# Residual rows by GpSimd gathers, and a register-addressed expert weight, in a two-stage attention and expert kernel

## The reference

```
x = x + delta_attention(layernorm(x))      # 16 heads of 8, a recurrence over the 512 tokens
x = x + experts(layernorm(x))
x = x + linear_attention(layernorm(x))     # 16 heads, chunks
x = x + experts(layernorm(x))

delta_attention:  q, k, v = silu(short_conv(x @ W)); q, k normalised per head
                  per token: v' = (v - k.S) * beta;  S += k (x) v';  o = q.S
                  o normalised per head, then @ Wo
experts:          gate = the two largest of softmax(x @ Wg), scaled to sum 1
                  y = sum over 8 experts of gate_e * (relu(x @ W1[e]) @ W2[e])   # 128 -> 256 -> 128
```

## Time and profile before

| | us |
|---|---|
| median of 3 runs (lowest, highest) | 939.39 (935.42, 940.16) |
| the profiled execution | 939.41 |
| its span | 937.6 |
| TensorE busy | 768.9 |
| VectorE busy | 645.5 |
| ScalarE busy | 540.8 |
| GpSimd busy | 394.9 |

### The profile page before, as it was taken

The page is one execution under the profiler, slowest core; times in us unless marked ns, Lnnn a source line. Parts: engine busy times, 40 slices in busy tenths (PEclk is TensorE's granted clock), DMA queues, the critical chain, the costliest instruction groups (busy, mean ns, idle before and its releaser), DMA issues.

```text
span 937.6 us, 17223 instructions
## 1 busy us (share of the span) xinstructions
PE 768.9 (82%) x5736; PEld 630.8 (67%) x5736; DVE 645.5 (69%) x1477; ACT 540.8 (58%) x1457; POOL 394.9 (42%) x433
## 2 busy tenths in 40 slices
PE   2653455888888899686888999999999999999997
PEld 1432233676666677574776787878787878787886
DVE  1146999899999999989854456565666574748350
ACT  5656446777877959464647454454535363636355
POOL 1065978597978889785561111111101010101012
PEclk9776667999999999789799999999999999999999
DMA  4223040403122030401010000000000000000000
GB/s 125 72 68 82 1 115 0 116 1 93 35 67 59 11 104 1 115 1 57 1 46 1 24 1 24 1 22 0 22 0 22 0 22 0 22 0 12 2 12 12
DMA packets 48446, 32.15 MB, mean 34 GB/s; under 512 B 37520, under 2 KB 38800, under 8 KB 48144
## 3 DMA queue, kind: packets, MB, share of 16 engines
q1 hardware_dynamic: 48400, 31.58, 12.1%
HBM read 18.73 MB, written 12.85 MB: 34 GB/s over the span
## 4 chain that ended last, share of the span: by engine, by line
PE 44%; DVE 28%; issue 8%; ACT 7%; POOL 5%; DMA 4%; SPq 2%; DVEq 0%; ACTq 0%; POOLq 0%
PE bank L1095 14%; PE bank L1241 6%; DVE u L1404 4%; PE bank L1073 4%; DVE hist_mem L1705 4%; DVE hist_mem L1413 4%; PE bank L1218 4%; PE bank L1075 3%; PE bank L1074 3%; DVE prod_mem L1397 3%; DVE hist_mem L1409 3%; POOL kk L473 2%; PE bank L1253 2%; DMA beta_p<-s_beta 2%; DVE x L1547 1%
## 5 line engine op out<-in xcount | busy, mean ns | idle before, releaser
L1095 PE MATMUL bank<-w,hid 128*128 128x128 f32 x2048 | 266.5, 286 | 30.5 <-DVE x L1547 9.0
L1095 PEld LDWEIGHTS bank<-w,hid 128*128 128x128 f32 x2048 | 256.9, 201 | 45.6 <-issue 33.1
L537 POOL TENSOR_TENSOR x_odd<-x_odd,y_odd 128x512 f32<-128x512 f32 x48 | 61.7, 1286 | 411.4 <-ACT y_odd L775 411.4
L740 ACT ACTIVATE hid<-bank 128x512 f32<-128x512 f32 x256 | 144.0, 600 | 97.1 <-PE bank L1075 94.2
L1073 PE MATMUL bank<-xT_h,w_h 128*128 128x512 f32 x256 | 115.2, 450 | 2.2 <-ACT hid L740 1.7
L1075 PE MATMUL bank<-xT_h,w_l 128*128 128x512 f32 x256 | 101.9, 398 | 0.0
L1074 PE MATMUL bank<-xT_l,w_h 128*128 128x512 f32 x256 | 101.6, 397 | 0.0
L522 POOL TENSOR_TENSOR oq_mem<-hist_mem,q_t 128x384 f32<-128x384 f32 (+1 forms) x96 | 101.4, 1089 | 0.0
L1404 DVE TENSOR_REDUCE u<-prod_mem 128x32 f32<-128x288 f32 x128 | 87.0, 679 | 3.3
L1005 PE MATMUL bank<-xnT_h,wtap_h 128*128 128x512 f32 x104 | 51.9, 499 | 35.3 <-DVE qkv L1369 21.1
L1712 DVE TENSOR_TENSOR prod_mem<-bank,causal 128x1024 f32<-128x1024 f32 x32 | 39.2, 1225 | 55.0 <-PE bank L1218 53.9
(11 more groups left out here) (169 smaller groups left out, 1501.8 us busy)
## 6 DMA issues: line engine op xcount, KB each, us to landing
s_qkv<-qkv SPq DMA_DIRECT2D x24, 256.0 KB, 3.6
pin<-s_qkv SPq DMA_DIRECT2D x16, 256.0 KB, 2.9
x_in<-in_x SPq DMA_DIRECT2D x8, 256.0 KB, 2.7
q_p<-s_qkv SPq DMA_DIRECT2D x8, 256.0 KB, 3.2
s_o<-o_p SPq DMA_DIRECT2D x8, 256.0 KB, 2.1
x_r<-in_x SPq DMA_DIRECT2D x8, 256.0 KB, 3.0
o_T<-s_o SPq DMA_DIRECT2D x8, 256.0 KB, 3.6
s_x<-x_odd SPq DMA_DIRECT2D x8, 256.0 KB, 2.4
```

What stands on the lines that cost most here:

```text
L740: nc.scalar.activation(hid[:, e % 2, f], bank[:, ZB + f, :], ACT.Relu).then_inc(hid_ready, 1)
L1095: last = nc.tensor.matmul(bank[:, y_bank(e, wide), tokens], hid[:, e % 2, f, tokens], w2[:, e, f], start=(f == 0), stop=(f == FC - 1))
```

## The change

The load of `x_r` for chunks 0 to 6 leaves SP. GpSimd issues four indirect transfers in its place, one for each block j of 128 rows, in a new function `fetch_residual`. Each takes its 128 row numbers from a column of the tile `row_at`, which an iota fills at the start. The call stands in GpSimd's step after `delta_solve(i + 1)` and before `delta_outputs(i, 0)`. `out_residual` waits for the four transfers of its chunk (argument `close`). The last chunk's `x_r` is still loaded by SP, on a semaphore of its own, `xr_last`. GpSimd's loop over steps 2 to 6 is written out.

In `moe_down` with `wide=False` TensorE first loads the expert's number from the tile `expert_at` in SBUF, filled by a second iota, into a register; the slice of `w2` is then addressed by that register. The values are the same as before: the number loaded for expert e is e. The semaphore `pool_ready` counts two more operations.

```diff
--- before.py
+++ after.py
@@ -178,6 +178,8 @@
 
         x_b = sb("x_b", [128, J, D])
         x_keep = x_in
+        row_at = sb("row_at", [128, NCH, J], mybir.dt.int32)
+        expert_at = sb("expert_at", [128, E], mybir.dt.int32)
         phi_min = sb("phi_min", [128, 2, NT])
         phi_k = sb("phi_k", [128, B, 2, CH])
 
@@ -239,7 +241,7 @@
 
         o_squared, o_norms, o_log = sem("o_squared"), sem("o_norms"), sem("o_log")
         o_rnorm, on_ready, o_projected = sem("o_rnorm"), sem("on_ready"), sem("o_projected")
-        xr_loaded = sem("xr_loaded")
+        xr_loaded, xr_last = sem("xr_loaded"), sem("xr_last")
 
         xr_ready, bnf_done, mvf_ready = sem("xr_ready"), sem("bnf_done"), sem("mvf_ready")
         rstdf_log, rstdf_ready, xf_ready = sem("rstdf_log"), sem("rstdf_ready"), sem("xf_ready")
@@ -270,7 +272,7 @@
                    (wv_b[:], d["wv_b"]), (wo_b[:], d["wo_b"]), (bo_rows[:], d["bo_rows"])]
         PREP_W = 5
 
-        POOL_ALL = 10
+        POOL_ALL = 12
         HALF = CH // 2
         FIRST = [i * (BS - 1) - i * (i - 1) // 2 for i in range(BS)]
         PRE_OPS = 2 + (BS - 1) + 2 * (BS - 1)
@@ -357,13 +359,14 @@
                 sp.wait_ge(go, 1)
                 if due(added_to):
                     sp.wait_ge(added, added_to)
-                sp.dma_start(x_r[:].rearrange("p j d -> p (j d)"), d["x"][c]).then_inc(xr_loaded, 16)
+                sp.dma_start(x_r[:].rearrange("p j d -> p (j d)"), d["x"][c]).then_inc(xr_last, 16)
 
             def heads_out(c):
 
                 heads_store(c)
                 heads_load(c)
-                load_xr(c)
+                if c == NCH - 1:
+                    load_xr(c)
 
             def store_mid(c):
                 this = held(sp, EV * (c + 1))
@@ -406,8 +409,6 @@
                     heads_store(o)
                 if i >= 3:
                     store_mid(i - 3)
-                if i:
-                    load_xr(o)
                 if ahead:
                     q_in(i + 1)
                 if i:
@@ -451,6 +452,11 @@
             pool.wait_ge(pool_ready, 8)
             for par in range(2):
                 nc.gpsimd.memset(v_bd[64 * par:64 * par + 64, :, :, par, HD], 1.0).then_inc(pool_ready, 1)
+
+            pool.wait_ge(pool_ready, 10)
+            nc.gpsimd.iota(row_at[:], pattern=[[128 * J, NCH], [1, J]], base=0, channel_multiplier=J).then_inc(pool_ready, 1)
+            pool.wait_ge(pool_ready, 11)
+            nc.gpsimd.iota(expert_at[:], pattern=[[1, E]], base=0, channel_multiplier=0).then_inc(pool_ready, 1)
 
             tt = nc.gpsimd.tensor_tensor
 
@@ -529,6 +535,16 @@
                 rows = oq.rearrange("p n j m d -> p (n j m) d")
                 tt(rows[:, :, HD // 2:HD], rows[:, :, 0:HD // 2], rows[:, :, HD // 2:HD], ALU.add).then_inc(o_part, 1)
 
+            def fetch_residual(c):
+
+                pool.wait_ge(pool_ready, POOL_ALL)
+                if c > 1:
+                    pool.wait_ge(added, EV * (c - 1) + 1)
+                for j in range(J):
+                    nc.gpsimd.indirect_dma_start(
+                        x_r[:, j], None, d["x"].rearrange("c p (j d) -> (c p j) d", j=J),
+                        bass.IndirectOffsetOnAxis(ap=row_at[:, c, j:j + 1], axis=0)).then_inc(xr_loaded, 16)
+
             def moe_add(n, e):
 
                 pool.wait_ge(odd_scaled, EV * n + e // 2 + 1)
@@ -549,6 +565,8 @@
                 if ahead:
                     delta_keys(i + 1)
                     delta_solve(i + 1)
+                if i:
+                    fetch_residual(i - 1)
                 delta_outputs(i, 0)
                 if moe:
                     moe_add(n, 3)
@@ -570,7 +588,7 @@
                 nc.gpsimd.memset(column[:, :, BS - 1, :, HD], 0.0).then_inc(oq_cleared, 1)
             step1(0, moe=False)
             step1(1, moe=False)
-            with pool.Fori(2, NCH - 1) as i:
+            for i in range(2, NCH - 1):
                 step1(i)
             step1(NCH - 1, ahead=False)
 
@@ -1077,6 +1095,7 @@
 
             def moe_down(n, e, wide=True, first=False):
 
+                at = e if wide else pe.value_load(expert_at[0:1, e:e + 1], min_val=0, max_val=E - 1)
                 pe.wait_ge(hid_ready, FC * (E * n + e + 1))
                 if e % 2 == 0 and wide and not first:
                     pe.wait_ge(even_scaled, scaled_even(n) + e // 2)
@@ -1092,7 +1111,8 @@
                 for j in range(J):
                     tokens = slice(128 * j, 128 * j + 128)
                     for f in range(FC):
-                        last = nc.tensor.matmul(bank[:, y_bank(e, wide), tokens], hid[:, e % 2, f, tokens], w2[:, e, f],
+                        weight = w2[:, e, f] if wide else w2[:, bass.ds(at, 1), f].rearrange("p o d -> p (o d)")
+                        last = nc.tensor.matmul(bank[:, y_bank(e, wide), tokens], hid[:, e % 2, f, tokens], weight,
                                                 start=(f == 0), stop=(f == FC - 1))
                 last.then_inc(y_part, 1)
 
@@ -1444,9 +1464,12 @@
                 dve.wait_ge(o_rnorm, c + 1)
                 tt(on[:], o_T[:], bank[:, MB, :], ALU.mult).then_inc(on_ready, 1)
 
-            def out_residual(c):
+            def out_residual(c, close=False):
                 dve.wait_ge(o_projected, c + 1)
-                dve.wait_ge(xr_loaded, 16 * (c + 1))
+                if close:
+                    dve.wait_ge(xr_loaded, 16 * J * (c + 1))
+                else:
+                    dve.wait_ge(xr_last, 16)
                 tt(x_r[:], x_r[:], bank[:, MB, :].rearrange("p (j d) -> p j d", j=J), ALU.add).then_inc(xr_ready, 1)
 
             def moe_xn(n, src, j):
@@ -1597,7 +1620,7 @@
                         out_on(o)
                 elif at == (7, 1):
                     if out:
-                        out_residual(o)
+                        out_residual(o, close=True)
                 elif at == (7, 3):
                     delta_qdot_sign(i)
                 elif at == (8, 0):
```

## The result

The changed kernel took 989.84 us (median of 4 runs, 989.44 to 992.66), the kernel before 938.00 beside it (4 runs, 935.42 to 940.16): 1.056 times as long, with an interval of 1.0523 to 1.0597. It is slower by 52 us. The profiled executions took 989.44 and 939.41 us with spans of 987.6 and 937.6, so 50.0 us of span are to be found.

The account below looks back on a forecast made before the run. VectorE's list of work was taken to bound the recurrent steps. Lag 13.2, transfers 38.4, sign flip -2.8, loads and clock 20 sum to 69 us on 939: 1008 us, slower by 7%, range 968 to 1056.

Parts of the forecast that it names:

- The place: GpSimd's list, steps 1 to 6: the fetch behind delta_solve is issued after VectorE wants the rows; 13.2 us together.
- The four transfers: Behind the solve, steps 1 to 6: 4.4 us issue plus 2.0 landing per step; 38.4 us (21.6 to 67.8).
- The sign flip: VectorE, steps 1 to 6: after the stall it no longer collides with GpSimd's solve; 2.8 us back.
- Not slower: Rival: VectorE's collisions with GpSimd go, 14 us back in six steps; 939 us or a little less; chance 0.03.
- SP's queue, the iotas: One issue less on SP, zero; two iotas at the start, covered by VectorE's wait for weights until 8.14 us.
- Loads and clock: TensorE, steps 2 to 7: register loads and half clock after the stall show at VectorE; 20 us (0 to 45).
- (a): Expert 0's load on TensorE, in a chain without idle time ahead of xnT_h: all of it shows, 1.0 us.
- The clock: TensorE idles some 7 us in the stall, then runs at half clock: 2.5 us of work takes 5.
- (c): Expert 4's product after the stall: 2.5 us of clock loss plus 1.0 load, less 1.0 room before VectorE's mix; 2.5 shows.
- Only the stall: Rival: register loads hide in TensorE's idle time and its clock holds; 988 us; chance 0.25, shared with cheap transfers.
- TensorE becomes the bound: Rival: each load stops the array for 2.4 us, none hidden; 1041 us; chance 0.19, shared with dear transfers.
- The wait isn't there: Rival: fetch issued before block 7, so no stall; excluded by GpSimd's order; part of the same few per cent.

## Why the prediction was right, and where not

The direction, the place and the mechanism were right, and the measured time is in the range; the time itself was 18 us too high. By its steps:

1. *The place.* Right. Lag in step 5: 2.25 us forecast, 2.07 measured.
2. *The four transfers.* Right. Forecast 4.4 of issue and 2.0 of landing; measured 4.87 with the gaps around them, and 1.73. The wait was said to be 8.6 us and is 8.8; six were said, and none in step 7 and before the last chunk, and that is so: 51.6 us forecast, 52.9 measured. The Trainium skill, "DMA: Bandwidth & Descriptors", section "Latency and other measured facts", has about 1 us to the first byte of a GpSimd transfer; the 0.95 us per issue agree with it, and with the gap of 0.30 the issues come 1.25 apart.
3. *The sign flip.* Right, 0.18 us throughout steps 1 to 7, 2.8 us back. That the picks and gates would give back another 3.1 was left to the rival *Not slower*.
4. and 5. *SP's queue, the iotas.* Right; the two iotas take 0.21 and 0.14 us and end at 4.1, ahead of 8.14.
6. *Loads and clock, 20 us.* This is the term that was mis-sized. In place of 20 us the waits for xnT_h and for the mixes grew by 3.6 + 2.4 = 6. The load: 1.0 us was taken, 0.64 is right. That it shows whole ahead of expert 0's product, (a), is wrong: in step 5 it shows with 0.23 on the weight loads and 0.05 on the matmuls. It was costed as if TensorE began it when the array is free; the sequencer begins it earlier. Register loads alone cost 2 us, and fixed addresses give nothing back. The clock: that it falls in the stall is right. Stretches of the changed kernel, the columns of the earlier trace rows:

```profile
391.00:395.40 4.40, 0.00 (x0) 0.00 (x0) 2.65 (x7) 1.99 (x11) 0.94 (x3) 0.50 0.06 15
395.40:399.40 4.00, 3.97 (x10) 3.15 (x11) 3.76 (x8) 3.94 (x18) 4.00 (x4) 0.52 0.00 0
399.40:403.40 4.00, 4.00 (x27) 3.58 (x26) 3.30 (x7) 3.67 (x9) 4.00 (x7) 1.00 0.00 0
```

TensorE is idle from 386.9 to 395.4. By the end of that it is at 0.50, the lower of its two levels (1.2 GHz); it stays there for most of its first 4 us of work (0.52) and has full clock in the next four. But the price was wrong. In TensorE's timeline the second projection, before and after, and the product of expert 4, which was to be late (before: 358.12):

```profile
353.74 0.51 PE L1005 MATMUL bank<-xnT_h,wtap_h 128*128 128x512 f32 x1 [0.38 <-DVE qkv L1369]
```

```profile
395.43 0.79 PE L1023 MATMUL bank<-xnT_h,wtap_h 128*128 128x512 f32 x1 [8.50 <-DVE qkv L1389]
...
401.45 1.95 PE L1115 MATMUL bank<-w,hid 128*128 x16
```

From one to the other it is 6.02 us, and was 4.38: 1.6 more, not 2.5. With a fixed address it is 6.13 (398.36 to 404.49), so no load is in it. The product itself is back at 1.95 us. Of the 1.6 the room of 1.0 hides one, and VectorE's mix waits 0.62:

```profile
403.52 1.13 DVE L1570 SCALAR_TENSOR_TENSOR x<-bank,gate_now,x 128x128 f32<-128x128 f32 x4 [0.62 <-PE bank L1115]
```

0.6 where (c) had 2.5, and 3.2 over all steps. The steps grew by 9.5 us (step 1) and 6.5 to 10.3 (2 to 6) where 8 and 11 to 12 were said. So the rival *Only the stall* (988 us) had the size, and half of its condition: the loads hide, but the clock does not hold. It fell, and the distance that VectorE keeps from TensorE took most of it up. That the measured 989.84 lies within 2 us of this rival's 988 is in part luck: 6 us of longer waits stand against 3.1 of fewer collisions and 1.4 of an earlier start.

*TensorE becomes the bound* is excluded: 0.64 us per load, not 2.4, and 0.04 of it in the time. Even eight loads per expert give 1083 us. *Not slower*: collisions do come and go, as it says, and in the change 3.1 us do beside the sign flip; its larger form was seen elsewhere, as a loss of some 11 us when the fetch was moved ahead of the solve. *The wait isn't there*: only with another place.

Open stay the 4.2 us before step 7 with the register weight everywhere, and some 3 of the 12 us of the early gathers.

## What to carry to other kernels

Ask of every transfer on a compute engine's queue what stands ahead of it in that list and who made that wait: here the fetch inherited a solve that starts on VectorE's own result, and the reader on VectorE came first. Count transfers, not bytes, where GpSimd issues them, and look for what the issues push: one early gather was nearly free, four early ones cost some 10 us more, most of it by moving GpSimd's work onto VectorE's. A register load costs what the sequencer's lead doesn't cover, which isn't the duration of the load.

## What the runs showed of the hardware

- GpSimd spent 0.94 to 0.99 us on issuing an indirect transfer of 128 rows, for 512 B and for 2 KB rows alike (1.13 on the first of all), 0.30 more before the next, and 0.58 on a plain one of 256 KB. From the end of the issue the data landed in 1.7 us (64 KB) and 2.4 us (256 KB).
- A load of a word from SBUF into TensorE's register took 0.30 us, 0.64 with what belongs to it. Alone it cost 0.04 us in the recurrent steps and about 0.1 where the kernel is bound by TensorE. The 16 matmuls behind it took 1.95 us at full clock, as with a fixed address.
- A small VectorE operation with both operands in SBUF took 2.83 us in the mean beside a busy GpSimd, 0.19 with one operand in PSUM. Five of six were held through several GpSimd operations in a row.
- At the end of an idle stretch of TensorE of 8.5 us its granted clock was 0.50, in the first 4 us of work behind it 0.52 and in the next four 1.00; from the projection to expert 4's product it took 1.6 us longer.
